# Expert loop of a fused transformer kernel: buffers by round, the weight split in two places, ScalarE in TensorE's order

## The reference

```
scores = softmax(h @ gate_w.T); topk_w, topk_ids = top_k(scores, 4); topk_w /= sum(topk_w)
buf[e, pos] = h[token]            # 32 experts, at most C = 2 * T * 4 / 32 = 512 rows each, more are dropped
g, u = split(buf @ w13[e]);  eo = (silu(g) * u) @ w2[e]
routed[token] += eo[e, pos] * weight
out = x + routed + silu(h @ shared_gate) * (h @ shared_up) @ shared_down
```

## Time and profile before

| | us |
|---|---|
| median of 3 runs | 1516.85 (1512.98 to 1518.78) |
| the profiled execution | 1516.78 |
| its span, first to last instruction | 1515.0 |
| PE busy | 1171.0 (77%) |
| PEld busy | 877.4 (58%) |
| DVE busy | 868.1 (57%) |
| ACT busy | 498.8 (33%) |
| POOL busy | 555.3 (37%) |

### The profile page before, as it was taken

One profiled execution on the slowest core, in us unless ns is written; L12 is line 12 of the kernel. 1 busy time (PEld: TensorE's weight loads), 2 busy tenths in 40 slices (PEclk: granted clock), 3 DMA queues, 4 the chain that ended last, 5 costly groups with the idle time before them and its releaser, 6 DMA issues. The chain is left out here.

```text
span 1515.0 us, 23393 instructions
## 1 busy us (share of the span) xinstructions
PE 1171.0 (77%) x6322; PEld 877.4 (58%) x6340; DVE 868.1 (57%) x1510; ACT 498.8 (33%) x1058; POOL 555.3 (37%) x589
## 2 busy tenths in 40 slices
PE   7998948668884818898539882549898889999967
PEld 6987625434442518788437661437666666666752
DVE  3253427468873616877535437955667656656625
ACT  2331411256662227676311110013333333333320
POOL 0000000011100100766841210037878878777850
PEclk9999969789997957887759996869999999999995
DMA  6112200000002666562040007046777876777549
GB/s 237 57 63 66 115 0 0 0 1 0 0 1 75 242 179 197 173 194 83 0 161 28 28 28 236 0 162 157 199 180 210 222 197 194 180 209 174 126 64 336
DMA packets 117315, 180.75 MB, mean 119 GB/s; under 512 B 13305, under 2 KB 48633, under 8 KB 117280
## 3 DMA queue, kind: packets, MB, share of 16 engines
q1 hardware_dynamic: 97040, 137.20, 27.2%
q0 software_dynamic: 18080, 38.85, 13.1%
q10 hardware_dynamic: 2160, 4.26, 0.8%
HBM read 138.37 MB, written 46.93 MB: 122 GB/s over the span
## 5 line engine op out<-in xcount | busy, mean ns | idle before, releaser
L204 POOL TENSOR_TENSOR ln_rstd<-ln_ve,powers 128x2 f32<-128x2 f32 (+1 forms) x40 | 25.8, 646 | 342.5 <-DVE ln_ve L198 342.5
L1958 POOL DMA_INDIRECT y_d<-x_eo,x_ox x80 | 130.5, 1631 | 35.4 <-issue 32.6
L2012 PE MATMUL x_h<-x_w_hi,x_t_hi 128*128 x320 | 126.4, 395 | 1.8 <-DVE x_t_lo L2112 1.8
L2013 PE MATMUL x_h<-x_w_lo,x_t_hi 128*128 x320 | 125.8, 393 | 0.0
L2014 PE MATMUL x_h<-x_w_hi,x_t_lo 128*128 x320 | 125.7, 393 | 0.0
L1943 POOL DMA_INDIRECT x_g<-r_d,x_ix x82 | 111.0, 1354 | 37.3 <-issue 36.1
L2112 DVE TENSOR_TENSOR x_w_lo<-w,x_w_hi (+1 forms) x64 | 109.3, 1748 | 0.0
L2031 PE MATMUL x_o<-x_w_hi,x_avt_hi 128*128 x160 | 76.0, 475 | 29.0 <-ACT x_avt_hi L2085 29.0
L2102 ACT COPY x_eo<-x_o 128x512 f32<-128x512 f32 x80 | 47.2, 589 | 127.5 <-DMA y_d<-x_eo,x_ox 118.6
L527 PE MATMUL p_bank<-wo,z_t 128*128 128x512 f32 x128 | 61.4, 636 | 34.2 <-DVE z_t L578 34.2
L1953 POOL COPY x_ox<-route 128x1 int32 (+1 forms) x80 | 82.0, 1025 | 0.9 <-DMA y_d<-x_eo,x_ox 0.6
(11 more groups left out here) (333 smaller groups left out, 2981.6 us busy)
## 6 DMA issues: line engine op xcount, KB each, us to landing
w<-in_L_ffn_w SPq DMA_DIRECT2D x32, 1024.0 KB, 5.4
h_negm<-negm_d SPq DMA_DIRECT2D x16, 1024.0 KB, 9.5
w<-in_L_ffn_w SPq DMA_DIRECT2D x32, 512.0 KB, 5.8
raw<-in_L_ffn_w SPq DMA_DIRECT2D x3, 2816.0 KB, 15.4
x_res<-in_x SPq DMA_DIRECT2D x8, 512.0 KB, 4.7
ctx_in<-in_ctx SPq DMA_DIRECT2D x8, 512.0 KB, 4.1
m_cx<-in_ctx SPq DMA_DIRECT2D x8, 512.0 KB, 4.0
qt_d<-m_qt SPq DMA_DIRECT2D x8, 512.0 KB, 4.6
```

Of the source, the lines that this page charges most:

```text
L1958: nc.gpsimd.indirect_dma_start(out=y_d[s], out_offset=bass.IndirectOffsetOnAxis(ap=ox[s][:], axis=0), in_=eo[s][:], in_offset=None, bounds ...
L2012: nc.tensor.matmul(hbank[s][:], hi[:, k, :], w13p[0][:, at, k, :], start=k == 0, stop=False)
L2013: nc.tensor.matmul(hbank[s][:], hi[:, k, :], w13p[1][:, at, k, :], start=False, stop=False)
```

## The change

In the expert loop:

- Gather buffers `xg`, index buffers `ix`, row buffers `ox` and output buffers `eo` exist twice, by the parity q of the round. The loop bodies hold two rounds, and the numbers of rounds are made even (`last_round` is shifted by 2).
- GpSimd only waits and issues. VectorE copies the indices at the start of a round, for two rounds later, and the scatter's rows near the end. The `carry` products are gone.
- VectorE rounds a weight where it split it before (`split_hi`), and subtracts in the next round between gated product 0 and the low part of activation 0 (`split_lo`). Each place reads the codes from memory again.
- ScalarE takes activation 1 ahead of x tile 1, and an output copy waits for the scatter of two rounds before.
- The last round turns no further x tiles.

In the routing block the transposes of `lost` are 4 in place of 16, to four groups of 32 partitions. In the combination `final` is loaded into the same four groups, and the four products of a chunk use one group each.

```diff
 ScalarE
                 turned_act(i, 0)
-                turned(i + 1, 0)
-                turned(i + 1, 1)
+                if more:
+                    turned(i + 1, 1 - q, 0)
                 turned_act(i, 1)
+                if more:
+                    turned(i + 1, 1 - q, 1)
                 for s in range(2):
                     act.wait_ge(eo_ps, OPEN + 2 * i + s + 1)
-                    if not first:
-                        act.wait_ge(added[s], 16 * i)
-                    nc.scalar.copy(eo[s][:], obank[s][:]).then_inc(eo_sb, 1)
+                    if before is not None:
+                        act.wait_ge(added[s], 16 * before)
+                    nc.scalar.copy(eo[q][s][:], obank[s][:]).then_inc(eo_sb, 1)
 VectorE
-            def split(e):
+            def split_hi(e):
                 at, raw = ds(e % SPLIT, 1), ds(e % 2, 1)
                 dve.wait_ge(w_ready, e + 1)
                 nc.vector.tensor_copy(w13p[0][:, at], w13[:, raw]).then_inc(w13_hi, 1)
                 nc.vector.tensor_copy(w2p[0][:, at], w2[:, raw]).then_inc(w2_hi, 1)
+            def split_lo(e):
+                at, raw = ds(e % SPLIT, 1), ds(e % 2, 1)
                 dve.wait_ge(w13_hi, e + 1)
                 lo_part(w13p[1][:, at], w13[:, raw], w13p[0][:, at]).then_inc(w13_lo, 1)
                 dve.wait_ge(w2_hi, e + 1)
                 lo_part(w2p[1][:, at], w2[:, raw], w2p[0][:, at]).then_inc(w2_lo, 1)
-            def at_first_unit(j, code):
+            def at_first_unit(code, part, j=None):
                 with dve.If(code < (NE - 2) * STRIDE):
                     with dve.If(code % STRIDE == 0):
-                        dve.wait_ge(eo_ps, OPEN + j)
-                        split(code // STRIDE + 2)
+                        if j is not None:
+                            dve.wait_ge(eo_ps, OPEN + j)
+                        part(code // STRIDE + 2)
+            def gather_rows(r, q):
+                nc.vector.tensor_copy(ix[q][:], route[:, 1, ds(2 * r, 2)]).then_inc(ix_ready, 1)
+            def scatter_rows(r, q, before):
+                if before is not None:
+                    for s in range(2):
+                        dve.wait_ge(added[s], 16 * before)
+                nc.vector.tensor_copy(ox[q][:], route[:, 0, ds(2 * r, 2)]).then_inc(ox_ready, 1)
+            def round_of(r, q, more=True, before=None):
+                if more:
+                    gather_rows(r + 2, q)
+                gated(r, 0)
+                for j in range(2) if not isinstance(r, int) or r else range(1, 2):
+                    at_first_unit(code_before(dve, 2 * r + j), split_lo)
+                turned_act(r, 0)
+                gated(r, 1)
+                if more:
+                    turned(r + 1, 0)
+                turned_act(r, 1)
+                if more:
+                    turned(r + 1, 1)
+                scatter_rows(r, q, before)
+                if more:
+                    for j in (2 * r + 1, 2 * r + 2):
+                        at_first_unit(code_of(dve, j), split_hi, j)
-            with dve.Fori(0, last_of(dve) + 1) as i:
-                codes_next = [code_of(dve, 2 * i + 1), code_of(dve, 2 * i + 2)]
 GpSimd
-                nc.gpsimd.tensor_copy(ix[:], route[:, 1, ds(2 * i, 2)]).then_inc(ix_ready, 1)
-                pool.wait_ge(ix_ready, i + 1)
-                nc.gpsimd.tensor_tensor(carry[:, 0:1], powers[:, 0:1], powers[:, 0:1], ALU.mult)
+                pool.wait_ge(ix_ready, r + 1)
+                if not isinstance(r, int) or r >= 2:
+                    pool.wait_ge(rw_ready, 2 * r - 2)
+            def round_of(r, q, more=True):
+                if more:
+                    gathers(r + 2, q)
+                scatter(r, q, 0)
+                scatter(r, q, 1)
 Combination
-            sp.dma_start(final[:, 0], y_d[0][T + P:, :]).then_inc(final_in, 16)
+            for g in range(R):
+                sp.dma_start(final[g * NE:(g + 1) * NE, 0], y_d[0][T + P:, :]).then_inc(final_in, 16)
...
-                    last = nc.tensor.matmul(lost_y[c % 2][:, t, :], lost_t[:, (c * R + t) * P:(c * R + t + 1) * P],
-                                            final[:, 0, :], start=True, stop=True)
+                    last = nc.tensor.matmul(lost_y[c % 2][:, t, :], lost_t[t * NE:(t + 1) * NE, c, :],
+                                            final[t * NE:(t + 1) * NE, 0, :], start=True, stop=True)
```

More of the change, by code:

```diff
@@ L1731, in _ @@
             nc.scalar.activation(ex[:], ex[:], ACT.Exp).then_inc(ex_ready, 1)
-            for h in range(NT // 4):
-                act.wait_ge(lost_ps, h + 1)
-                nc.scalar.copy(lost_t[:, 4 * h * P:4 * (h + 1) * P], lost_bank[h % 2][:]).then_inc(lost_sb, 1)
+            act.wait_ge(lost_ps, 1)
+            nc.scalar.copy(lost_t[:], lost_bank[:])
         @block.tensor
@@ L1750, in _ @@
             for h in range(NT // 4):
[L1751 to L1755, removed]
+                last = nc.tensor.transpose(lost_bank[:, h, :], lost[:, 4 * h:4 * h + 4, :].rearrange("p t e -> p (t e)"), ident[:])
+            last.then_inc(lost_ps, 1)
             with pe.Fori(0, NT // 2) as i:
@@ L1928, in _ @@
         def _(pool):
[L1930 to L1934, removed]
-                if not first:
-                    pool.wait_ge(rw_ready, 2 * i)
-                nc.gpsimd.tensor_copy(ix[:], route[:, 1, ds(2 * i, 2)]).then_inc(ix_ready, 1)
-                pool.wait_ge(ix_ready, i + 1)
-                nc.gpsimd.tensor_tensor(carry[:, 0:1], powers[:, 0:1], powers[:, 0:1], ALU.mult)
+            for q in range(2):
+                for s in range(2):
+                    nc.gpsimd.memset(xg[q][s][:], 0.0).then_inc(fills, 1)
@@ L2063, in _, with turned @@
             with pe.Fori(0, n) as i:
-                rest(i, experts_of(i), experts_of(i + 1))
-            rest(n, experts_of(n))
+                for q in range(2):
+                    rest(i, q, experts_of(2 * i + q), experts_of(2 * i + q + 1))
+            rest(n, 0, experts_of(2 * n), experts_of(2 * n + 1))
+            rest(n, 1, experts_of(2 * n + 1))
         @block.scalar
         def _(act):
-            def turned(i, s, first=False):
+            def turned(i, q, s, first=False):
                 j = 2 * i + s
@@ L2087, in _, with round_of @@
             act.sem_inc(eo_sb, OPEN)
-            turned(0, 0, first=True)
-            turned(0, 1, first=True)
-            def round_of(i, first=False):
+            turned(0, 0, 0, first=True)
+            turned(0, 0, 1, first=True)
+            def round_of(i, q, more=True, before=None):
                 silu(i, 0)
@@ L2166, in experts @@
+            split_lo(1)
+            at_first_unit(code_of(dve, 0), split_hi, 0)
+            n = last_of(dve)
+            round_of(0, 0)
+            round_of(1, 1)
+            with dve.Fori(0, n - 1) as i:
+                round_of(2 * i + 2, 0, before=2 * i + 1)
+                round_of(2 * i + 3, 1, before=2 * i + 2)
+            for s in range(2):
+                dve.wait_ge(added[s], 32 * n)
+            round_of(2 * n, 0)
+            round_of(2 * n + 1, 1, more=False)
     with ExitStack() as sc:
@@ L2193, in _ @@
         def _(act):
-            act.dma_start(final[:, 1], y_d[1][T + P:, :]).then_inc(final_in, 16)
+            for g in range(R):
+                act.dma_start(final[g * NE:(g + 1) * NE, 1], y_d[1][T + P:, :]).then_inc(final_in, 16)
             for c in range(CH):
```

132 lines of the change are left out of this document (68 added, 64 removed).

## The result

| | before | after |
|---|---|---|
| median of the runs beside each other | 1516.18 us (4 runs, 1512.98 to 1518.78) | 1573.14 us (4 runs, 1563.52 to 1576.65) |
| ratio, with its 95% interval | | 1.037 (1.032 to 1.042) |
| the profiled execution, its span | 1516.78, 1515.0 | 1576.65, 1574.8 |
| start of the first round to start of the last | 454.5 | 509.9 |

The direction was forecast, the size was not: 57 us slower where 16 were expected. Nearly all of it lies in the loop. Of the 59.8 us between the two profiled spans, 55.4 are the loop; 3.6 are a later start of it, and 0.8 lie behind the start of the last round (60.0 us after, 59.2 before).

What follows compares the result with a forecast made beforehand. The expert loop bounds the kernel, TensorE at full clock but stalling on gated products and ScalarE's order. Terms summed to +8.4 us at full clock, plus 8 for clock falls: 1533 us, range 1498 to 1553.

Steps and rivals of the forecast that it cites:

- late rounds: Nineteen loop rounds splitting a weight on the second tile; forecast from 11.76 to 12.7 us each, +17.8 in all.
- no-split rounds: Loop rounds that split no weight; eight forecast from 10.62 to 9.83 us each, -6.3 in all.
- ScalarE's order: Second activation ahead of the second x tile removes most of TensorE's 0.98 us stall; 0.79 per no-split round, -6.3.
- Output buffers: Two output buffers end ScalarE's 118.6 us of scatter waits, but TensorE waits for none of it; costed at nothing.
- The split in two places: First gated product at 3.59, then x, then 3.41 us of subtractions delay the second; round 10.16 + x.
- The early kind: Nine loop rounds splitting a weight on the first tile; forecast from 10.89 to 11.6 us each, +6.6 in all.
- x: Time from the first gated product's issue to the first subtraction: 1.45 us early, 2.5 late, bounds 0.4 and 3.5.
- The clock: TensorE idles about 3 us in late rounds; six of nineteen lose the clock at 1.4 us each, +8.
- Rival D: Clock falls in most late rounds and half-speed down matmuls lengthen the next too; +35, 1552 us; chance 0.15.
- the last round's -2: The last round turns no unused tile and issues scatters without GpSimd's copies and products; -2 us.
- Gathers: Gathers two rounds ahead remove one round's 4.26 us TensorE wait; that round becomes 11.6 us, -6.0.
- The tail: After the loop, products in four row groups fall below the loads, -1.4; six more loads give back 1.1; sum -0.3.

Runs made afterwards that it cites:

- e6: The kernel before with ScalarE's order alone changed: second tile's turned activations ahead of the next round's second row tile; 1490.4 us, recorded ratio 0.989.
- e4: The changed kernel with the weight split whole again at the end of the round and the codes read at the round's top; 1490.9 us, ratio 0.983.
- e2: The changed kernel with eight extra unused matmuls per round in TensorE's idle stretch, ahead of the second tile's transposes; 1560.7 us, ratio 1.030.
- e3: The changed kernel with the last two rounds waiting only for the scatters of the round before last, as the loop's rounds do; 1567.2 us, ratio 1.036.
- e11: e2 with two more unused reads of unit codes behind gated 0, ahead of the two there; 1633.3 us, ratio 1.078.
- e7: e4 plus e3's waits, with w2's low part moved behind the next round's gated 0, its codes read ahead and the following codes behind; 1471.0 us, ratio 0.971.
- e10: e7 with the next round's codes read ahead of gated 0 too, leaving no read behind it; 1507.8 us, ratio 0.994.
- e1: The changed kernel with VectorE's two reads of the unit codes moved ahead of gated 0, low parts still behind it; 1539.3 us, ratio 1.016.
- e9: The kernel before with the split in two places alone, single buffers and ScalarE's old order kept; 1601.3 us, ratio 1.056.
- e8: e4 plus e3's waits, with ScalarE's old order put back and the buffers by round kept; 1510.7 us, ratio 0.996.

## Why the prediction was wrong

Between the forecast's +16.4 us and the +59.8 of the profiled executions lie 43.4. The late rounds have 27.5 of them: 53.3 in place of 17.8 and 8 of clock, which is 18 for the clock and 9 for the round at full clock. The round before the last has 5.9, the other no-split rounds 3.3, the last round with the tail 3.1; the rest is under 2 us a term.

**ScalarE's order.** Right in mechanism, and wrong in where it pays. I gave 0.79 us to each of eight no-split rounds, and nothing to the rounds with a split apart from their own formula. In e6 the no-split rounds gained only 0.37 on the mean (10.63 to 10.26; the fastest came to 9.86), but the late ones 0.78 (11.76 to 10.98) and the early ones 0.58: 26 us with the second round and the rest. That swap was the gain to be had, and the two places took back three times as much.

**Output buffers.** Costed at nothing, and right: ScalarE's 118.6 us of waiting went and moved next to nothing (e6 keeps that wait, 120.1 us, and its kinds of rounds have means within 0.2 of e4's).

**The split in two places: the start of gated 0.** The early kind was right: 11.73 against 11.6. The late kind's term was the step that failed first, 12.7 against 13.18 at full clock. What failed in it was not x, the time from gated 0 to the first subtraction, which was 2.18 where 2.5 was forecast. It was the 3.59 in front of x. The prediction wrote of the rounding that "it still ends near 4.4, before the subtractions' 6.1: no further cost". It ended there, but the first gated product stands behind it on VectorE, and started at 4.44. That is 0.85 more, less 0.32 of x: 0.5 a round, and 19 x 0.5 = 9 us. That x came out near its middle value owes something to luck, for single reads ran from 0.30 to 0.95.

**The clock.** The larger error. I took six falls of 1.4 us. Seventeen of the nineteen late rounds lost the clock, and only two (13.19, 13.23) did not. The seventeen are 1.55 us longer than 13.18 on the mean, from 0.5 to 2.6, so the price was near and the count was not. Rival D's mechanism held, with 26 us in place of my 8. The Trainium skill (TensorE: Matmul & The Clock Gate, "Why this matters for your kernels") spoke for D, and the trace agrees: 17 of 19 fell, behind stretches of 2.8 to 3.8 us without weight loads. I had set against it that TensorE is busy before and after each gap; that did not protect these. D's 1552 was missed by the term above, by the next one and by the no-split rounds.

**The drain.** Not in the prediction at all. The wait `added[s] >= 32 * n` ahead of round 2n asks for every scatter issued so far, where the loop's rounds ask for those of two rounds before. It holds ScalarE and VectorE for 8 us and the round for 5.1 (7.8 in e4). It stood in the code that I priced as the last round's -2.

**Gathers.** 17.69 to 13.31 in place of 11.6. The wait is gone, but this round too lost the clock, behind 2.20 us without weight loads (0.50 in the window 1278.40 to 1281.05); at full clock it is 11.77 to 11.78 (e2, e3): right. The start was 3.6 later where I said 1.5; this lies within what the start moves by itself.

**The tail.** -0.3 forecast; from the last round's start to the end it is +0.8, together with the -2 of the last round that did not come. The 1.39 us stall went as I said, and the loads set the end. Sixteen products take 3.53 us (granted clock 0.56) where half of 27.67 was 13.8 (0.50): 3.9 times as fast, and no use here. The Trainium skill (TensorE: Matmul & The Clock Gate, Part 3) has 3.07 for four row tiles; this trace shows more. My own figure from the earlier trace rows, 2.20 us in place of 5.1, gives 12 us for the 32 products and not the 13 that I wrote.

By the rounds that the prediction named, 9.8, 11.6 and 12.7 us, the second kind holds at full clock (11.69 the fastest), the first nearly (10.03; e6 has 9.86), and the third does not. In the kernels with the loop of two rounds the up products take 5.60 us in place of 5.49; no run shows why. The starts of the second gated product were forecast at 7.0, 8.7 and 9.8; at full clock they came at 7.1, 8.8 and 10.3.

## What to carry to other kernels

A register read from memory cost here what the engine behind it was not covering. Behind gated 0, where VectorE's queue was empty, two more reads with their preparation stood on the path in full (1.0 us each, e11). The same reads ahead of gated 0 were hidden beneath the 2.29 us of a low part when there were two of them (e7), were not when there were four (e10), and cost 0.9 us where no long instruction lay over them (e1's early rounds). So place a read by what runs above it, and count all the reads together.

A term can be right in its end and still cost: the rounding ended where it was forecast, but what stood behind it in VectorE's order had been placed earlier. Check each new start against the instruction ahead of it on the same engine.

When work is moved into the middle of another engine's chain, add up what that engine is going to stand still for, and price the clock for every such stretch near the length at which the trace has shown a fall, not for a share of them. Look for waits in peeled last iterations that ask for more than the loop's own. And try each part of a bundle by itself: here a swap of two lines was worth 26 us, and the rest of the change hid it.

## What the runs showed of the hardware

- A read of one integer into a VectorE register is 0.31 us at the median, but 0.45 or more in 5 of 81 cases before, 23 of 158 after and 60 of 238 in e11 (up to 1.0). On TensorE's side the same read was that long in 1 of 160 cases before and in none of 160 in e6, but in 41 of 160 after, and in 26 to 51 of 160 in the other kernels whose loop body holds two rounds. The longer body is not the whole of it: e9, with one round in the body, has 16 on TensorE and 34 of 160 on VectorE. What makes a read long stays open.
- Stretches of 3.50 and 3.60 us without weight loads ended once with the clock at 0.50 and once at 1.00; the length alone does not decide it there. Of the nineteen late rounds of after two kept the full clock, behind 3.60 and 3.65 us, and in e2, with at most 1.73 us, all did. After's nine early rounds kept it behind 2.1 to 2.2 us, but the round of the gather lost it behind 2.20.
- Open: why the no-split rounds stay at 10.1 to 10.3 in several kernels where 9.95 is possible, and at 11.16 in e8. I tried no kernel on either.
